# Message stage of two graph layers: weights and the lane row read from PSUM, two sum banks, add ahead of the product

## The chip, the cores and the metric

The kernel runs on one core of one Trainium2 chip. The metric is the device time of one execution in microseconds; lower is better. The core has five engines that run side by side and wait for each other through semaphores: TensorE (PE, its weight loads PEld), VectorE (DVE), ScalarE (ACT), GpSimd (POOL) and SyncE (SP). SBUF and PSUM are its memories of 128 partitions.

## The reference

The model runs four layers over 2500 nodes with 256 features: a graph attention layer (4 heads), a mixture of experts, a graph transformer layer (8 heads) and a second mixture. The two graph layers use 80,000 edges, sorted by destination. What this case touches is the last step of each graph layer: every edge takes its source's row, scales each head's part by the edge's attention weight, and the results are summed per destination.

```python
ex = jnp.exp(scores - m[edge_dst])                 # layer 0, 4 heads of 64
denom = jax.ops.segment_sum(ex, edge_dst, num_segments=N)
alpha = ex / jnp.maximum(denom[edge_dst], 1e-09)
msg = alpha[:, :, None] * h[edge_src]
agg = jax.ops.segment_sum(msg, edge_dst, num_segments=N)
# layer 1, 8 heads of 32, the same with a self loop on each node
msg = Vh[src] * a[:, :, None]
attn = jax.ops.segment_sum(msg, dst, num_segments=N).reshape(N, D_MODEL)
```

## The kernel before, in words

Edges are cut into 157 groups of 512 (four tiles of 128 edges, one edge on a partition), nodes into 20 tiles of 128. Because the edges are sorted, a group touches one node tile or a few; the pairs of group and tile form a staircase of NS = 176 steps, and a table `s.steps` tells each step its ring slot, tile and group. The table row of a node holds 256 values and a one behind each head (D + H = 260 or 264 columns), so that the denominators are summed along; the division comes later.

`pass_messages` is the message stage, once for each graph layer (in layer 0 `most` is None, in layer 1 it holds each node's self loop weight). Its engines:

- GpSimd (`gather_quad`, L731) fetches table rows with indirect DMAs (L756), 128 rows each, eight to a quad (two groups). A ring holds 8 quads (RQ). For quad q it waits at L1034 until the product of the last step on quad q - 8 has been made. Seven quads (layer 0) or eight (layer 1) are gathered before the stage starts. In the ring turns 1 to 5 (layer 0) or 1 to 8 (layer 1) every second quad isn't gathered: it was gathered during the score stage (`gather_ahead`, L795) and stored in HBM, and SyncE loads it with one DMA (L1057). The offsets of a gather lie in SBUF (`g.index`).
- SyncE (`report`) waits for landed rows (L1063) and tells VectorE through `rows_landed`.
- VectorE, for step n: the one-hots `pick` of the four tiles (L1094: destination minus tile base, compared with the row 0..127; 512 columns), a wait for the rows, the product `msg` (L1098: ring rows times weights; 1040 or 1056 columns), and then the add of the sums of step n - LATE (LATE = 2) from PSUM into `acc` in SBUF (L1107: 260 or 272 columns).
- TensorE multiplies one-hots by messages, four fp32 matmuls a step (L1121), into one of DEPTH = 3 PSUM banks `ps_m`.
- ScalarE, in layer 1 only, copies the self loop weights into the tail of `msg` (L1077).

`pick` and `msg` have three buffers each. `staged` unrolls the steps six at a time. In layer 0 the weights lie in spare columns of `xn` (tile name all_xn), in layer 1 in a tensor of their own (e_weight). `lane_row`, `dst_col` and `tile_base` lie in SBUF.

## Time and profile before

| | us |
|---|---|
| median of 3 runs | 3143.92 |
| lowest, highest run | 3139.3, 3148.53 |
| profiled execution | 3144.7 |
| its span, first to last instruction | 3142.8 |
| message stage of layer 0, first one-hot to the next stage's first VectorE instruction | 554.23 to 1202.80 |
| message stage of layer 1, likewise | 2287.20 to 2817.53 |
| busy in the whole span: PE, DVE, ACT, POOL | 1798.8, 1769.9, 368.8, 1701.8 |
| mean granted TensorE clock, as a share of 2.4 GHz | 0.764 |

The profile is one execution. A timeline line gives start and duration in us, the engine, the line of the kernel, the operation and what it writes and reads; in brackets stands the engine's idle time before it and what ended it. A group line gives the count, the busy time in us, the mean of one in ns, and the idle time before its members. "issue" is time in which the engine waited for nothing that the profile shows.

### The profile page before, as it was taken

How to read it: one execution, taken by the hardware profiler on the slowest of the kernel's cores; microseconds unless marked ns; L12 is line 12 of the kernel's file. 1: busy time of each engine (PE TensorE's matmuls, PEld its weight loads, DVE VectorE, ACT ScalarE, POOL GpSimd, SP SyncE). 2: the span in 40 equal slices, each digit the busy share in tenths (PEclk: the TensorE clock that was granted, in tenths of full speed). 3: DMA queues.
4: the chain of work that ended last, by engine and by line, in shares of the span. 5: the costliest groups of instructions: out<-in, count | busy, mean ns of one | idle time of the engine just before them, and what ended most of it. 6: DMA issues, size and time to landing. Idle time of an engine off the chain costs nothing. (4 is left out here: it accounts for less than half of the span.)

```text
span 3142.8 us, 35335 instructions
## 1 busy us (share of the span) xinstructions
PE 1798.8 (57%) x10362; PEld 1444.4 (46%) x10362; DVE 1769.9 (56%) x2713; ACT 368.8 (12%) x715; POOL 1701.8 (54%) x1504
## 2 busy tenths in 40 slices
PE   2301292777755553999741112693177777756668
PEld 2200182555544442799740000693155555535557
DVE  6200098867644447455730000699787777757756
ACT  1100001000000001445200000000300000004244
POOL 3577606887877775000047777205878788761010
PEclk8655596888877776899865555797588888878889
DMA  3355553455433332000135566433145554430000
GB/s 121 119 190 189 173 184 95 126 160 162 136 92 92 92 91 74 1 1 0 63 89 196 196 200 198 148 117 112 54 146 165 162 165 162 134 115 8 4 31 34
DMA packets 140778, 361.01 MB, mean 115 GB/s; under 512 B 39352, under 2 KB 65360, under 8 KB 126890
## 3 DMA queue, kind: packets, MB, share of 16 engines
q0 software_dynamic: 69760, 225.91, 24.0%
q1 hardware_dynamic: 65866, 122.18, 11.2%
q10 hardware_dynamic: 5088, 12.13, 1.1%
q8 instruction: 32, 0.52, 0.1%
q14 instruction: 32, 0.26, 0.0%
HBM read 289.00 MB, written 71.12 MB: 115 GB/s over the span
## 5 line engine op out<-in xcount | busy, mean ns | idle before, releaser
L756 POOL DMA_INDIRECT e_ring<-table,e_index x840 | 1101.4, 1311 | 369.7 <-issue 255.5
L1121 PE MATMUL ms_ps_m<-ms_msg,ms_pick 128*128 128x260 f32 (+1 forms) x2816 | 830.4, 461 | 373.0 <-issue 258.2
L1121 PEld LDWEIGHTS ms_ps_m<-ms_msg,ms_pick 128*128 128x128 f32 x2816 | 634.4, 230 | 568.8 <-issue 432.3
L657 PE MATMUL sc_ps_e<-sc_keys,sc_hot 125*128 125x100 bf16 (+1 forms) x3840 | 353.7, 240 | 569.5 <-issue 561.3
L620 DVE TENSOR_REDUCE all_xn<-sc_ps_e 128x800 f32 (+1 forms) x240 | 234.1, 1019 | 633.7 <-remote 527.8
L657 PEld LDWEIGHTS sc_ps_e<-sc_keys,sc_hot 125*128 125x128 bf16 x3840 | 272.7, 102 | 650.3 <-issue 633.3
L795 POOL DMA_INDIRECT all_acc<-table,e_stage_index x416 | 397.1, 955 | 142.4 <-issue 141.1
L1098 DVE TENSOR_TENSOR ms_msg<-e_ring,all_xn 128x1040 f32 x176 | 218.0, 1239 | 254.1 <-SPq L1063 135.6
L1098 DVE TENSOR_TENSOR ms_msg<-e_ring,e_weight 128x1056 f32 x176 | 220.9, 1255 | 128.1 <-SPq L1063 112.7
L1094 DVE SCALAR_TENSOR_TENSOR ms_pick<-graph_dst_col,graph_tile_base,graph_lane_row 128x512 f32<-128x512 f32 x352 | 263.7, 749 | 12.0 <-issue 9.8
L1107 DVE TENSOR_TENSOR all_acc<-all_acc,ms_ps_m 128x260 f32 (+1 forms) x352 | 150.3, 427 | 8.3 <-PE ms_ps_m L1121 8.0
L131 POOL TENSOR_TENSOR w_qkv_low<-w_qkv,w_qkv_high 128x1536 fp32r<-128x1536 f32 x1 | 3.7, 3657 | 278.4 <-ACT w_qkv_high L126 278.4
L887 ACT ACTIVATE all_acc<-wt_ps_t 128x512 f32<-128x512 f32 x15 | 8.0, 624 | 1001.4 <-PE wt_ps_t L860 1001.3
L131 DVE TENSOR_TENSOR moe_hidden_low<-all_acc,moe_hidden_high 128x512 fp32r<-128x512 f32 x80 | 55.2, 692 | 94.7 <-ACT moe_hidden_high L126 94.7
L728 POOL COPY e_index<-graph_src_col 128x32 int32 (+1 forms) x40 | 14.4, 359 | 158.1 <-SPq L847 158.0
L1077 ACT ACTIVATE ms_msg<-e_dst_line 128x32 f32 x176 | 40.6, 231 | 499.8 <-PE ms_ps_m L1121 433.9
L140 PE MATMUL moe_ps_y<-moe_w_high,moe_hidden_high 128*128 128x256 f32 x320 | 91.4, 286 | 1.9 <-DVE moe_hidden_low L131 1.9
L140 PE MATMUL moe_ps_y<-moe_w_high,moe_hidden_low 128*128 128x256 f32 x320 | 91.6, 286 | 0.0
L140 PE MATMUL moe_ps_y<-moe_w_low,moe_hidden_high 128*128 128x256 f32 x320 | 91.5, 286 | 0.0
L419 ACT ACT_TABLE_LOAD x3 | 3.8, 1283 | 680.8 <-PEq L1142 670.8
L614 DVE TENSOR_SCALAR sc_hot<-sc_rows,all_node_of 125x1024 bf16<-125x1024 bf16 x160 | 80.7, 506 | 4.3 <-DMA sc_rows<-src_low 4.1
L446 PE MATMUL ln_ps_t<-all_ident,all_xn 128*128 128x128 f32 x160 | 31.2, 365 | 85.9 <-DVE all_xn L409 78.0
(415 smaller groups left out, 2682.0 us busy)
## 6 DMA issues: line engine op xcount, KB each, us to landing
ahead<-all_acc POOLq DMA_DIRECT2D x32, 1056.0 KB
e_ring<-ahead SPq DMA_DIRECT2D x32, 1056.0 KB
sc_rows<-src_low SPq DMA_DIRECT2D x160, 200.0 KB
ahead<-all_acc POOLq DMA_DIRECT2D x20, 1040.0 KB
e_ring<-ahead SPq DMA_DIRECT2D x20, 1040.0 KB
e_ring<-table,e_index POOLq DMA_INDIRECT x840
sc_rows<-src_high ACTq DMA_DIRECT2D x160, 50.0 KB
all_acc<-table,e_stage_index POOLq DMA_INDIRECT x416
```

What stands on the lines that cost most here:

```text
L131: return dve.tensor_tensor(low, value, high.bitcast(F32), ALU.subtract)
L140: product = pe.matmul(out, a, b, start=first and i == 0, stop=last and i == len(products) - 1)
L614: dve.tensor_scalar(hot[0:KEYS, q, :], rows[0:KEYS, q, :], s.node_of[0:KEYS, 0:1], None, ALU.is_equal).then_inc(hot_ready, 1)
L620: dve.tensor_reduce(edge[:, bass.ds(it * ITEM + sub * SL, SL), :], found, AX.X, ALU.max).then_inc(picked, 1)
L657: mm = pe.matmul(ps_e[lane][:, t * SLOT:t * SLOT + C], hot[0:KEYS, q, cols], keys[0:KEYS, part, :, :].rearrange("p g h -> p (g h)"), start ...
L756: pool.indirect_dma_start(out=g.ring[:, slot * QUAD + i // GT, i % GT, :], out_offset=None, in_=s.table[:, :], in_offset=bass.IndirectOffs ...
L795: pool.indirect_dma_start(out=stage.rows[:, b, t, :], out_offset=None, in_=s.table[:, :], in_offset=bass.IndirectOffsetOnAxis(ap=stage.ind ...
L1077: act.activation(msg[:, b, :, R:W], most[:, bass.ds(group * GT, GT), :], ACT.Copy).then_inc(tail_ready, 1)
L1094: dve.scalar_tensor_tensor(out=pick[:, b, :, :], in0=s.dst_col[:, bass.ds(group * GT, GT)].unsqueeze(2).broadcast_to([P, GT, P]), scalar=s ...
L1098: dve.tensor_tensor(msg[:, b, :, 0:R].rearrange("p t (h o) -> p t h o", h=H), ring[:, bass.ds(slot, 1), :, :].rearrange("p a t (h o) -> p ...
L1107: dve.tensor_tensor(into, into, ps_m[(b - LATE) % DEPTH][:, 0:W], ALU.add).then_inc(added, 1)
L1121: mm = pe.matmul(ps_m[b][:, 0:W], pick[:, b, t, :], msg[:, b, t, :], start=t == 0, stop=t == GT - 1)
```

## The change

The row 0..127 is copied once into a PSUM bank (`ps_lane`) by ScalarE, and the one-hots read it there. In layer 0 ScalarE copies all weights (2560 columns, five banks) into PSUM once; in layer 1, where they don't fit, it copies those of each step (32 columns) into one of three banks, ahead of its tail copy, and VectorE waits for them (`weight_set`). Products read the weights there. The sums use two banks in place of three. VectorE's step becomes one-hots, add of step n - 2, wait for rows, product. `iteration` now gets the step's position in the unrolled loop (q), from which buffer b = q % DEPTH and bank q % BANKS follow.

```diff
--- before.py
+++ after.py
@@ -978,7 +978,13 @@
         ring, row_in, order = g.ring, g.row_in, g.order
         pick = m.sb("pick", [P, DEPTH, GT, P])
         msg = m.sb("msg", [P, DEPTH, GT, W])
-        ps_m = [m.ps(f"ps_m{i}", [P, 512]) for i in range(DEPTH)]
+        BANKS = 2
+        ps_m = [m.ps(f"ps_m{i}", [P, 512]) for i in range(BANKS)]
+
+        ps_lane = m.ps("ps_lane", [P, 512])
+        lane_row = ps_lane[:, 0:P]
+        ps_w = m.ps("ps_w", [P, ET, H]) if most is None else [m.ps(f"ps_w{i}", [P, 512]) for i in range(DEPTH)]
+        near_set, weight_set = m.sem("near_set"), m.sem("weight_set")
         rows_landed, ahead_in, loaded, most_kept = m.sem("rows_landed"), m.sem("ahead_in"), m.sem("loaded"), m.sem("most_kept")
         acc_zero, tail_ready, pick_ready, msg_ready, summed, added = (
             m.sem(n) for n in ("acc_zero", "tail_ready", "pick_ready", "msg_ready", "summed", "added"))
@@ -1016,12 +1022,12 @@
             unroll = 2 * DEPTH
             first = DEPTH + (NS - DEPTH) % unroll
             for n in range(first):
-                iteration(n, n % DEPTH, n)
+                iteration(n, n, n)
             with eng.Fori(0, (NS - first) // unroll) as turn:
                 for q in range(unroll):
-                    iteration(turn * unroll + (first + q), (first + q) % DEPTH, None)
+                    iteration(turn * unroll + (first + q), first + q, None)
             for n in range(NS, last):
-                iteration(n, n % DEPTH, n)
+                iteration(n, n, n)
 
         def later(fixed, than):
 
@@ -1070,13 +1076,18 @@
 
             @block.scalar
             def _(act):
-                def iteration(n, b, fixed):
+                def iteration(n, q, fixed):
+                    b = q % DEPTH
                     (group,) = step_values(ENG.Activation, n, slice(2, 3), (NG - 1,))
                     if later(fixed, DEPTH):
                         act.wait_ge(summed, n - (DEPTH - 1))
+                    act.activation(ps_w[b][:, 0:GT * H].rearrange("p (t h) -> p t h", h=H), weight[:, bass.ds(group * GT, GT), :], ACT.Copy).then_inc(weight_set, 1)
                     act.activation(msg[:, b, :, R:W], most[:, bass.ds(group * GT, GT), :], ACT.Copy).then_inc(tail_ready, 1)
 
-                if most is not None:
+                act.activation(lane_row, s.lane_row[:, :], ACT.Copy).then_inc(near_set, 1)
+                if most is None:
+                    act.activation(ps_w[:, :, :], weight[:, :, :], ACT.Copy).then_inc(weight_set, 1)
+                else:
                     act.wait_ge(most_kept, 1)
                     staged(act, iteration, NS)
 
@@ -1086,39 +1097,50 @@
                 if most is not None:
                     dve.tensor_tensor(most, most, s.is_last[:, :].unsqueeze(2).broadcast_to([P, ET, H]), ALU.mult).then_inc(most_kept, 1)
                 dve.wait_ge(acc_zero, 2)
-
-                def iteration(n, b, fixed):
+                dve.wait_ge(near_set, 1)
+                if most is None:
+                    dve.wait_ge(weight_set, 1)
+
+                def iteration(n, q, fixed):
+                    b = q % DEPTH
                     slot, tile, group, tile_late = step_values(ENG.DVE, n, slice(0, 4), (RING - 1, NT - 1, NG - 1, NT - 1))
                     if fixed is None or fixed < NS:
 
                         dve.scalar_tensor_tensor(out=pick[:, b, :, :], in0=s.dst_col[:, bass.ds(group * GT, GT)].unsqueeze(2).broadcast_to([P, GT, P]),
-                                                 scalar=s.tile_base[:, bass.ds(tile, 1)], in1=s.lane_row[:, :].unsqueeze(1).broadcast_to([P, GT, P]),
+                                                 scalar=s.tile_base[:, bass.ds(tile, 1)], in1=lane_row.unsqueeze(1).broadcast_to([P, GT, P]),
                                                  op0=ALU.subtract, op1=ALU.is_equal).then_inc(pick_ready, 1)
-                        dve.wait_ge(rows_landed, group + 1)
-                        dve.tensor_tensor(msg[:, b, :, 0:R].rearrange("p t (h o) -> p t h o", h=H),
-                                          ring[:, bass.ds(slot, 1), :, :].rearrange("p a t (h o) -> p (a t) h o", h=H),
-                                          weight[:, bass.ds(group * GT, GT), :].unsqueeze(3).broadcast_to([P, GT, H, O + 1]), ALU.mult).then_inc(msg_ready, 1)
                     if later(fixed, LATE):
 
                         dve.wait_ge(summed, n - (LATE - 1))
                         if later(fixed, LATE + 1):
                             dve.wait_ge(added, n - LATE)
                         into = acc[:, bass.ds(tile_late, 1), 0:W].rearrange("p a w -> p (a w)")
-                        dve.tensor_tensor(into, into, ps_m[(b - LATE) % DEPTH][:, 0:W], ALU.add).then_inc(added, 1)
+                        dve.tensor_tensor(into, into, ps_m[(q - LATE) % BANKS][:, 0:W], ALU.add).then_inc(added, 1)
+                    if fixed is None or fixed < NS:
+                        dve.wait_ge(rows_landed, group + 1)
+                        if most is None:
+                            shares = ps_w[:, bass.ds(group * GT, GT), :]
+                        else:
+                            dve.wait_ge(weight_set, n + 1)
+                            shares = ps_w[b][:, 0:GT * H].rearrange("p (t h) -> p t h", h=H)
+                        dve.tensor_tensor(msg[:, b, :, 0:R].rearrange("p t (h o) -> p t h o", h=H),
+                                          ring[:, bass.ds(slot, 1), :, :].rearrange("p a t (h o) -> p (a t) h o", h=H),
+                                          shares.unsqueeze(3).broadcast_to([P, GT, H, O + 1]), ALU.mult).then_inc(msg_ready, 1)
 
                 staged(dve, iteration, NS + LATE)
 
             @block.tensor
             def _(pe):
-                def iteration(n, b, fixed):
+                def iteration(n, q, fixed):
+                    b = q % DEPTH
                     pe.wait_ge(pick_ready, n + 1)
                     pe.wait_ge(msg_ready, n + 1)
                     if TAILS:
                         pe.wait_ge(tail_ready, n + 1)
-                    if later(fixed, DEPTH):
-                        pe.wait_ge(added, n - (DEPTH - 1))
+                    if later(fixed, BANKS):
+                        pe.wait_ge(added, n - (BANKS - 1))
                     for t in range(GT):
-                        mm = pe.matmul(ps_m[b][:, 0:W], pick[:, b, t, :], msg[:, b, t, :], start=t == 0, stop=t == GT - 1)
+                        mm = pe.matmul(ps_m[q % BANKS][:, 0:W], pick[:, b, t, :], msg[:, b, t, :], start=t == 0, stop=t == GT - 1)
                     mm.then_inc(summed, 1)
 
                 staged(pe, iteration, NS)
```

## Rows read from the trace of the kernel before

**Rows 1.** the page, part 5: out<-in xcount | busy us, mean ns | idle before it

```profile
L795 POOL DMA_INDIRECT all_acc<-table,e_stage_index x416 | 397.1, 955 | 142.4 <-issue 141.1
```

**Rows 2.** groups by line, 550 to 1203 us, message stage of layer 0

```profile
L756 POOL DMA_INDIRECT e_ring<-table,e_index x412 | 512.3, 1244 | 125.1 <-issue 124.4 <-DMA e_ring<-table,e_index 0.6
L1121 PE MATMUL ms_ps_m<-ms_msg,ms_pick 128*128 128x260 f32 x1408 | 427.9, 473 | 225.7 <-issue 135.7 <-DVE ms_msg L1098 56.3 <-DVE all_acc L1107 33.1
...
L1098 DVE TENSOR_TENSOR ms_msg<-e_ring,all_xn 128x1040 f32 x176 | 218.0, 1239 | 254.1 <-SPq L1063 135.6 <-issue 118.5
L1094 DVE SCALAR_TENSOR_TENSOR ms_pick<-graph_dst_col,graph_tile_base,graph_lane_row 128x512 f32<-128x512 f32 x176 | 131.8, 749 | 5.9 <-issue 4.3 <-DVE all_acc L1085 0.8
L1107 DVE TENSOR_TENSOR all_acc<-all_acc,ms_ps_m 128x260 f32 x176 | 74.1, 421 | 3.2 <-PE ms_ps_m L1121 3.1
```

**Rows 3.** the same for 2287 to 2820 us, message stage of layer 1

```profile
L756 POOL DMA_INDIRECT e_ring<-table,e_index x308 | 417.8, 1357 | 105.7 <-issue 94.9 <-DVE ms_msg L1098 10.5 <-DMA e_ring<-table,e_index 0.3
...
L1098 DVE TENSOR_TENSOR ms_msg<-e_ring,e_weight 128x1056 f32 x176 | 220.9, 1255 | 128.1 <-SPq L1063 112.7 <-issue 15.3
...
L1107 DVE TENSOR_TENSOR all_acc<-all_acc,ms_ps_m 128x272 f32 x176 | 76.3, 433 | 5.1 <-PE ms_ps_m L1121 4.9
```

**Rows 4.** timeline (start us, us, engine, line) of one stretch of layer 0

```profile
700.93 0.75 DVE L1094 SCALAR_TENSOR_TENSOR ms_pick<-graph_dst_col,graph_tile_base,graph_lane_row 128x512 f32<-128x512 f32 x1
701.59 1.24 DVE L1098 TENSOR_TENSOR ms_msg<-e_ring,all_xn 128x1040 f32 x1
701.81 1.85 POOL L756 DMA_INDIRECT e_ring<-table,e_index  x1 [0.30 <-issue]
...
703.08 0.75 DVE L1094 SCALAR_TENSOR_TENSOR ms_pick<-graph_dst_col,graph_tile_base,graph_lane_row 128x512 f32<-128x512 f32 x1
703.96 0.94 POOL L756 DMA_INDIRECT e_ring<-table,e_index  x1 [0.30 <-issue]
705.21 0.95 POOL L756 DMA_INDIRECT e_ring<-table,e_index  x1 [0.30 <-issue]
```

**Rows 5.** timeline: a gather that begins inside a one-hot, one inside an add

```profile
764.55 0.75 DVE L1094 SCALAR_TENSOR_TENSOR ms_pick<-graph_dst_col,graph_tile_base,graph_lane_row 128x512 f32<-128x512 f32 x1 [0.46 <-issue]
764.88 1.24 POOL L756 DMA_INDIRECT e_ring<-table,e_index  x1 [0.30 <-issue]
...
766.37 0.42 DVE L1107 TENSOR_TENSOR all_acc<-all_acc,ms_ps_m 128x260 f32 x1
766.43 0.95 POOL L756 DMA_INDIRECT e_ring<-table,e_index  x1 [0.30 <-issue]
```

**Rows 6.** groups of VectorE by shape, whole span

```profile
L957 DVE SCALAR_TENSOR_TENSOR all_xn<-e_dst_line,all_xn 128x2560 f32<-128x2560 f32 x2 | 9.6, 4797 | 0.1
...
L1629 DVE SCALAR_TENSOR_TENSOR all_acc<-dense_ps,w_b,all_acc 128x512 f32<-128x512 f32 x10 | 7.5, 750 | 8.9 <-PE dense_ps L140 8.9
```

**Rows 7.** stretches: us, busy us of each engine (instructions), granted clock, DMA share, GB/s

```profile
570.00:600.00 30.00, 26.76 (x108) 19.14 (x106) 27.70 (x39) 0.00 (x0) 25.87 (x16) 1.00 0.41 134
554.00:850.00 296.00, 222.90 (x816) 176.42 (x817) 224.02 (x308) 0.00 (x0) 242.29 (x184) 0.86 0.48 150
1810.00:1980.00 170.00, 32.28 (x110) 11.72 (x110) 12.05 (x15) 0.00 (x0) 126.63 (x151) 0.50 0.62 199
```

**Rows 8.** one line: duration ns min/median/max, first and last start

```profile
L891 ACT ACTIVATE all_acc<-all_acc x3: 2337/2339/2339, 541.1 to 2257.7; 128x2560 f32<-128x2560 f32 x3
```

**Rows 9.** timeline of ScalarE in layer 1, backlogged TensorE ahead of it

```profile
2297.02 0.23 ACT L1077 ACTIVATE ms_msg<-e_dst_line 128x32 f32 x1 [1.60 <-PE ms_ps_m L1121]
```

**Rows 10.** timeline: the end of the message stage of layer 0

```profile
1192.43 1.85 POOL L756 DMA_INDIRECT e_ring<-table,e_index  x1 [0.31 <-issue]
...
1202.80 0.24 DVE L1146 TENSOR_SCALAR fin_inv<-all_acc 128x80 f32<-128x80 f32 x1 [0.50 <-PEq L1030]
```

**Rows 11.** timeline: the end of the message stage of layer 1

```profile
2807.11 1.87 POOL L756 DMA_INDIRECT e_ring<-table,e_index  x1 [0.30 <-issue]
...
2817.53 0.24 DVE L1544 TENSOR_SCALAR dense_loop<-all_score 128x160 f32<-128x160 f32 x1 [0.33 <-PEq L1030]
```

## The prediction

> **What bounds the kernel now.** Read the groups by line of the two message stages first, then a stretch of the timeline, then the two ends. A stage has 176 steps; VectorE spends 0.75 us of each on one-hots, 1.24 or 1.26 on the product and 0.42 on the add, and sits idle 254 us (layer 0) and 128 us (layer 1) before products, mostly until SyncE reports landed rows (L1063) [rows 2, 3]. So rows come too slowly, and these come from GpSimd's indirect gathers at L756: 412 of them in layer 0, 308 in layer 1, with only 0.30 us between two [rows 2 to 4]. GpSimd is never out of work: its idle time is that issue gap, and once 10.5 us for a ring place [rows 2, 3]. It sets the end of both stages: the last gather ends at 1192.43 + 1.85 = 1194.28, 8.5 us before the next stage's first VectorE instruction, and at 2807.11 + 1.87 = 2808.98, also 8.5 us before it [rows 10, 11].
>
> The gathers themselves are slow here. They take 1.244 us and 1.357 us on average, where the same kind of instruction takes 0.955 us in the score stages [rows 1 to 3]. The timeline says which are slow. The one at 701.81 begins inside a product and ends at 703.66, which is 0.83 us after that product's end (701.59 + 1.24); the two behind it, with VectorE idle, take 0.94 and 0.95 [rows 4]. One that begins inside a one-hot ends at 766.12, 0.82 us after it; one that begins 0.06 us into an add takes 0.95 [rows 5]; of 19 that begin inside an add none is longer than 0.98. So a gather needs something at its start that a product or a one-hot holds to its end and an add does not. Product and one-hot read two tensors from SBUF; the add reads one from SBUF and one from PSUM. While VectorE works without pause, each 2.15 us step (700.93 to 703.08) holds one gather of 1.85 + 0.30 us [rows 4]: both are locked together, though a free gather needs 0.95 + 0.30 = 1.25 us.
>
> **Part 1, the second operand moves to PSUM (one-hot: lane row; product: weights).** If the held thing is what the second SBUF tensor takes, all gathers fall to 0.955 us. Layer 0: 512.3 − 412 × 0.955 = 118.8 us. Layer 1: 417.8 − 308 × 0.955 = 123.7 us. The issue gaps stay. The sum, 242.5 us, comes off the path if GpSimd still sets both ends.
>
> Does it? In layer 0 its last gather would end at 1194.3 − 118.8 = 1075.5, while VectorE needs 176 × 2.15 = 378 us from 554 on, so 143 us are to spare. In layer 1 it would end at 2685.3 and the stage 8.5 us later at 2693.8. VectorE's step there is 2.15 + 0.016 + 0.012 = 2.18 us (longer product and add), so 384 us from 2287.2, with some 6 us of issue gaps as in layer 0 [rows 2, 3], and about 6 us for the last sums: 2683. Only 11 us are left, and the ring ties the two, as a gather waits for the product eight quads back. Every second quad comes from the HBM copy until turn 8, so a quad pair costs GpSimd 8 × 1.26 = 10.1 us and VectorE, at 176/157 steps a group, 4.5 × 2.18 = 9.8. I charge 4 us for stalls of this tie (0 if they never meet, 11 if VectorE sets the end).
>
> Does an operand in PSUM make VectorE slower? For 260 columns the add, with a PSUM operand, takes 421 ns; for 1040 the product, without, takes 1239: 1.05 ns a column, and the same 150 ns fixed [rows 2]. The one-hot has its twin at L1629: 512 columns, a per-partition scalar, one tensor in PSUM, 750 ns against 749 [rows 2, 6]. So nothing. By the Trainium skill (VectorE: DVE Perf Modes, section on the TRN2 errata) an instruction that reads PSUM pays 120 cycles where one from SBUF pays 58, so 65 ns more, twice a step; by that table layer 1's step would be 2.31 us and the stage end at 2706. The trace does not agree: its pairs differ by 1 ns.
>
> What no row shows is a PSUM operand that repeats each value (the weights, 65 or 33 times over). Lower bound: no extra. Upper bound: the strided read at L957, 4797 ns for 2560 columns, 1.81 ns a column after 150 fixed [rows 6]; for the product that is +0.79 us. I take nothing, since the product already repeats the weights from SBUF at 1.05.
>
> **Part 2, ScalarE's copies into PSUM.** Layer 0: one copy of 2560 columns at 2.34 us [rows 8] beside the two engines' memsets, ahead of the first one-hot at 554; hidden. If ScalarE began late, at most 2.3 us once. Layer 1: 176 copies of 16 to 32 columns, near the tail copy's 0.23 us. ScalarE has 1.60 us of idle even while TensorE steps at 0.23 + 1.60 = 1.83 us [rows 9]. The first product waits for one more copy: 0.4 us. Later ones need step n − 3 summed; the product of n comes 5.3 us after that of n − 3 ended, against 1.83 for the sums and 0.5 for both copies. Uncovered, they would put 0.2 us on each step.
>
> **Part 3, the order one-hot, add, product.** No instruction is added on VectorE but one wait. Behind the add's wait for the sums of n − 2 now stand the product and, through it, TensorE, the ring place and GpSimd. From the end of product n − 2 to that add lie one-hot, add and product of n − 1 and the one-hot of n: 2.15 + 0.66 − 0.09 = 2.7 us. The sums take 1.83 plus some 0.2: 0.6 us spare. Before, the product lay between as well, 1.15 us more. In return the add no longer stands behind the wait for rows, and TensorE's 33 us of waiting for adds in layer 0 [rows 2] go; they hide behind the gathers, so nothing.
>
> **Part 4, two banks.** TensorE's step n waits for add n − 2, which VectorE now does before product n, and TensorE waits for that anyway. Nothing. The faster gathers raise the traffic: 184 gathers in 296 us made 150 GB/s at a DMA share of 0.48 [rows 7]; at 1.26 us it becomes some 210 GB/s. The score stage ran 199 GB/s at 0.62 with gathers undisturbed at 0.955 [rows 1, 7]. Nothing.
>
> **Sum.** 118.8 + 123.7 − 4 − 0.4 = 238 us. The profiled run took 3144.7 us (span 3142.8), so 2906.7; the median of the runs is 0.8 below it: 2906 us. Within the case 2890 (no stalls, gathers at 0.945 us, 5 us of spread between runs) to 2920 (the full 11 for the tie, ScalarE's 2.3, the spread).
>
> **Rivals.**
> A. One-hots still hold the gathers, since the per-partition scalar is read from SBUF beside dst_col. Then in unbroken work two steps (4.30 us) hold three gathers, 1.43 us each, +0.18. Alternating turns: 160 + 256 gathers, 75 us; the rest, one one-hot a step with half of them met for 0.3 us, 15 us. GpSimd's slowness then gives VectorE pauses, so about 80: 2986. For: a pointer is an SBUF read. Against: it is 128 single values, in about 60 ns (749 against 512 × 1.04 + 150).
> B. A PSUM read costs VectorE something fixed. Up to 0.06 us a step (11/176) it hides in layer 1; twice that, 0.12 us, puts VectorE's end at 2704, 10 us past GpSimd's where I charged 4: 2912. Against: the pairs above. The skill's table named there is this case.
> C. The sums come late. TensorE's granted clock is 1.00 in unbroken work and 0.86 over the busy part of layer 0 [rows 7], full and half rate (2.4 and 1.2 GHz) mixed, after gaps without rows. At half rate a step is twice 1.83, 1.8 us too many, of which 0.6 are spare. If this hits once in every six steps of layer 1: 29 × 1.2 = 35, less the 11 spare, in place of the 4: 2926. Against: the gaps go as gathers speed up.
> D. The product's repeated PSUM read runs at the strided rate: step 2.15 + 0.79 = 2.94 us, VectorE sets both ends. Layer 0: 176 × 2.94 + 12 = 529 us for now 648.6; layer 1: 535 for 530.3. Together −115: 3029.
> E. Slower than before: both repeated operands run at 1.81 or worse. One-hot +0.39 too, step 3.33 us in layer 0, 3.36 in layer 1: 598 + 603 = 1201 us against 1179, so 3166. It decides from a step of 3.28 us, 1.1 more than now. Against: both repeat from SBUF at full rate.
> F. The change doesn't do what it says: what blocks is the long write or the length of the product, not its second SBUF input. Then 3144. Against: the one-hot, only 0.75 us, holds a gather to its end, and the add holds none.
>
> **Chances.** Forecast 0.72, A 0.10, B 0.03, C 0.04, D 0.04, E 0.04, F 0.03. The range from 2890 takes in A and ends at 2990; D, E and F stay out, 0.11. Less than 0.3% (9 us) is about what a measurement of this kernel can't tell from nothing. Faster: 0.93; same: 0.03 (F); slower: 0.04 (E).
>
> **What would show it.** Gathers at L756 with a mean near 0.955 and hardly any above 1.0; 40 of them in 50 us where now 31 stand; last gathers near 1075 and, counted from the start of layer 1's stage, near 398 us in. Product 1.24 and one-hot 0.75 unchanged (B, D, E if not). Idle before the product in layer 0 small until about 780 us, then 5 us a quad; in layer 1 close to none before the product and little before the add (C if much). Slow gathers that end 0.82 us after a one-hot are A, after a product F. I am wrong outright if gathers are short and the stages still don't shrink: then DMA landing sets the pace.

## The result

The changed kernel took 3301.5 us (median of four, 3290 to 3311), the kernel before 3142.9 us beside it: a ratio of 1.050, interval 1.046 to 1.054. The forecast was 2906 us. One thing must be known for all that follows: one and the same kernel before took some 3140 us in the runs of the result and in those around f1_after, t2_mixed and u1_dose below (*starved* runs from here on), and 2937 us around all other experiments (*free* runs). In free runs the changed kernel takes 2689 us, 8.5% less than the kernel before (2937.1). So the sign of the change hangs on the kind, and the forecast was made from a starved profile.

The page of the changed kernel, part 5 (columns as in [rows 1]; "remote" is a signal whose sender the profile couldn't tell):

```profile
L756 POOL DMA_INDIRECT e_ring<-table,e_index x840 | 854.7, 1018 | 724.9 <-DVE ms_msg L1126 354.4
L1143 PE MATMUL ms_ps_m<-ms_msg,ms_pick 128*128 128x260 f32 (+1 forms) x2816 | 821.8, 446 | 547.5 <-DVE ms_msg L1126 303.5
...
L657 PE MATMUL sc_ps_e<-sc_keys,sc_hot 125*128 125x100 bf16 (+1 forms) x3840 | 351.9, 238 | 575.3 <-issue 564.2
L620 DVE TENSOR_REDUCE all_xn<-sc_ps_e 128x800 f32 (+1 forms) x240 | 230.0, 984 | 635.2 <-remote 417.7
...
L1118 DVE TENSOR_TENSOR all_acc<-all_acc,ms_ps_m 128x260 f32 (+1 forms) x352 | 150.6, 428 | 569.1 <-remote 295.0
L1126 DVE TENSOR_TENSOR ms_msg<-e_ring,ms_ps_w 128x1040 f32 (+1 forms) x352 | 436.2, 1239 | 0.6 <-ACT ms_ps_w L1084 0.4
L1109 DVE SCALAR_TENSOR_TENSOR ms_pick<-graph_dst_col,graph_tile_base,ms_ps_lane 128x512 f32<-128x512 f32 x352 | 261.0, 742 | 0.8 <-DVE all_acc L1096 0.8
```

The same page of the kernel before has for the gathers:

```profile
L756 POOL DMA_INDIRECT e_ring<-table,e_index x840 | 1101.4, 1311 | 369.7 <-issue 255.5 <-SPq L847 101.9 <-DVE ms_msg L1098 10.5
```

The change did to the instructions what it was meant to do. Gathers fell from 1311 to 1018 ns on average, the product still takes 1239, the one-hot 742 (749 in [rows 2]). What is new is 569 us of VectorE idle ahead of the add, and 354 us in which GpSimd waits for products: the ring is full. Groups by line of layer 0's message stage (the same view as [rows 2]):

```profile
L756 POOL DMA_INDIRECT e_ring<-table,e_index x412 | 391.2, 950 | 294.7 <-DVE ms_msg L1126 172.3 <-issue 121.9 <-DMA e_ring<-table,e_index 0.3
...
L1126 DVE TENSOR_TENSOR ms_msg<-e_ring,ms_ps_w 128x1040 f32 x176 | 216.6, 1231 | 0.2 <-issue 0.2
...
L1118 DVE TENSOR_TENSOR all_acc<-all_acc,ms_ps_m 128x260 f32 x176 | 74.3, 422 | 343.9 <-remote 295.0 <-PE ms_ps_m L1143 48.2 <-issue 0.7
```

The wait ahead of the product went from 254.1 us [rows 2] to 0.2, the one ahead of the add from 3.2 to 343.9. The stage grew from 648.1 to 728.8 us (first one-hot to end of last add), layer 1's from 530.0 to 614.6, where the same two waits went from 128.1 to 0.4 and from 5.1 to 225.1 [rows 3]. The two stages make 165 of the 167 us between the spans (3309.8 and 3142.8). A stretch of the timeline shows one such wait (lines left out at the dots):

```profile
996.54 1.91 PE L1143 MATMUL ms_ps_m<-ms_msg,ms_pick 128*128 128x260 f32 x8 [2.36 <-DVE ms_msg L1126]
...
1004.01 1.23 DVE L1126 TENSOR_TENSOR ms_msg<-e_ring,ms_ps_w 128x1040 f32 x1
...
1005.47 3.81 PE L1143 MATMUL ms_ps_m<-ms_msg,ms_pick 128*128 128x260 f32 x8 [7.02 <-DVE ms_msg L1126]
1006.02 0.94 POOL L756 DMA_INDIRECT e_ring<-table,e_index  x1 [1.05 <-DVE ms_msg L1126]
1007.27 0.95 POOL L756 DMA_INDIRECT e_ring<-table,e_index  x1 [0.30 <-issue]
...
1014.79 0.95 POOL L756 DMA_INDIRECT e_ring<-table,e_index  x1 [0.30 <-issue]
1016.99 0.43 DVE L1118 TENSOR_TENSOR all_acc<-all_acc,ms_ps_m 128x260 f32 x1 [11.09 <-remote]
```

The add at 1016.99 takes the sums of the step whose matmuls start at 996.54; as modelled they end at 998.45. VectorE gets their signal 18.4 us later, when GpSimd's series of eight gathers, started 1.25 us apart from 1006.02 on, is over, and stands still for 11.09 us of that; behind the add stand the product, the ring place and GpSimd. The trace has kept the time of 160 of layer 0's 176 signals. Of these, 46 came more than 5 us after the last matmul's modelled end, on average 11.9 and at most 21.6 us: 30 while GpSimd stood still after a series, 16 while gathers still went on. In the kernel before, none of the 323 signals kept in its two message stages came more than 3.5 us late. Since the ends are modelled, the traces don't tell whether the last matmuls or only their signal is late.

### The profile page after: what moved, and what is told of

Its sections match the earlier page's. It is cut to its first block and busy times, and to the rows that moved or that the text cites. A ratio compares the mean times of both kernels' runs of the same rounds, so it can differ in the third digit from the quotient of the medians.

```text
span 3309.8 us, 35845 instructions
## 1 busy us (share of the span) xinstructions
PE 1786.6 (54%) x10362; PEld 1397.2 (42%) x10362; DVE 1768.5 (53%) x2713; ACT 392.2 (12%) x894; POOL 1455.2 (44%) x1504
## 5 line engine op out<-in xcount | busy, mean ns | idle before, releaser
L756 POOL DMA_INDIRECT e_ring<-table,e_index x840 | 854.7, 1018 | 724.9 <-DVE ms_msg L1126 354.4
L1143 PE MATMUL ms_ps_m<-ms_msg,ms_pick 128*128 128x260 f32 (+1 forms) x2816 | 821.8, 446 | 547.5 <-DVE ms_msg L1126 303.5
L1143 PEld LDWEIGHTS ms_ps_m<-ms_msg,ms_pick 128*128 128x128 f32 x2816 | 592.9, 219 | 776.0 <-issue 664.5
L1126 DVE TENSOR_TENSOR ms_msg<-e_ring,ms_ps_w 128x1040 f32 (+1 forms) x352 | 436.2, 1239 | 0.6 <-ACT ms_ps_w L1084 0.4
L1109 DVE SCALAR_TENSOR_TENSOR ms_pick<-graph_dst_col,graph_tile_base,ms_ps_lane 128x512 f32<-128x512 f32 x352 | 261.0, 742 | 0.8 <-DVE all_acc L1096 0.8
L1084 ACT ACTIVATE ms_ps_w<-e_weight 128x32 f32 x176 | 35.4, 201 | 554.5 <-PE ms_ps_m L1143 277.3
L1342 ACT ACTIVATE all_acc<-moe_ps_h,moe_bias 128x512 f32<-128x512 f32 x80 | 55.1, 689 | 119.8 <-PE moe_ps_h L140 119.1
```

What stands on the lines that cost most here:

```text
L756: pool.indirect_dma_start(out=g.ring[:, slot * QUAD + i // GT, i % GT, :], out_offset=None, in_=s.table[:, :], in_offset=bass.IndirectOffs ...
L1109: dve.scalar_tensor_tensor(out=pick[:, b, :, :], in0=s.dst_col[:, bass.ds(group * GT, GT)].unsqueeze(2).broadcast_to([P, GT, P]), scalar=s ...
L1126: dve.tensor_tensor(msg[:, b, :, 0:R].rearrange("p t (h o) -> p t h o", h=H), ring[:, bass.ds(slot, 1), :, :].rearrange("p a t (h o) -> p ...
L1143: mm = pe.matmul(ps_m[q % BANKS][:, 0:W], pick[:, b, t, :], msg[:, b, t, :], start=t == 0, stop=t == GT - 1)
L1342: act.activation(hidden[:, slot, f, :], ps_h[slot * KB + f][:, :], ACT.Gelu, bias=bias[:, j, f:f + 1]).then_inc(hidden_kept, 1)
```

## The experiments

Three theories of the late sums came first. Theory G: gathers that follow each other without a break delay the others' signals, and in the kernel before the products had kept such series short. Theory O: the new order leaves the sums too little room. Theory B: two banks do. The code below is cut to the lines that matter; lines that only rename or set up are left out.

**One part at a time.** e1_order is the kernel before with the add put between one-hot and product (operands in SBUF, three banks). In this cut `product` and `add` stand for their instructions and waits.

```diff
-    product(n); if later(fixed, LATE): add(n - LATE)
+    if later(fixed, LATE): add(n - LATE)
+    product(n)
```

> The kernel before with the new order alone: one-hot, add, product; both operands still in SBUF, three banks. Theory G (free-running gathers delay the sums; products that hold the gathers protected them): the gathers are still held, so the sums come on time and the time stays at 3143 us within 15. Rival O (the order leaves the sums too little room, whatever the gathers do): slower by 60 us or more, VectorE idle ahead of the add.

e2_banks is the kernel before with two banks.

```diff
-        ps_m = [m.ps(f"ps_m{i}", [P, 512]) for i in range(DEPTH)]
+        BANKS = 2
+        ps_m = [m.ps(f"ps_m{i}", [P, 512]) for i in range(BANKS)]
```

> The kernel before with two banks for the sums in place of three, old order, operands in SBUF. Theory G: 3143 us within 15, since TensorE's step waits for an add that comes 0.43 us after the product. Rival B (two banks tie TensorE to VectorE and that makes the sums late): slower by 60 us or more, TensorE idle for the add.

e3_psum is the changed kernel with the product ahead of the add again, the diff above backwards.

> The changed kernel with the old order (one-hot, product, add of two steps before), operands in PSUM, two banks. Theory G: the gathers run free as in the changed kernel (mean about 1.02 us), the sums of the two stages come late in bursts again, and the time stays above 3200 us. Rival O: about 2906 us, what was forecast, since only the order was wrong.

e4_lane is the kernel before with only the row 0..127 in PSUM.

```diff
-                 in1=s.lane_row[:, :].unsqueeze(1).broadcast_to([P, GT, P]),
+                 in1=lane_row.unsqueeze(1).broadcast_to([P, GT, P]),
```

> The kernel before with only the row 0..127 in PSUM: one-hots no longer hold the gathers, products still do; old order, three banks. Theory G: gathers are shorter than 1.25 us and still throttled by one product a step; some gain is left, 3060 to 3143 us, and the sums are late in few places. Rival O and rival B: the same gain, no more late sums than before; should the time rise above 3160, even this much freedom of the gathers costs more than it gives.

Measured, all four beside 2936.5 us for the kernel before, free runs:

| kernel | us | ratio, interval |
|---|---|---|
| e1_order | 2923.7 | 0.9953, 0.9935 to 0.9971 |
| e2_banks | 2930.4 | 0.9982, 0.9971 to 0.9992 |
| e3_psum | 2691.9 | 0.9165, 0.9147 to 0.9182 |
| e4_lane | 2929.4 | 0.9977, 0.9965 to 0.9989 |

O and B fall for free runs: neither order nor banks cost anything, the order gains 13 us. Theory G as I had put it, with late sums and over 3200 us for e3_psum, falls too: its gathers run free and its sums are on time (4.5 and 4.0 us of idle ahead of the adds). The gain needs the weights in PSUM: with the row alone the gathers stay at 1229 and 1371 ns and 7 us are gained, where I had expected up to 83. With VectorE at work each gather of e4_lane still begins inside a product and ends 0.8 us after it: one at 601.87 takes 1.84 us, beside a product at 601.66 of 1.23.

The surprise was the 2936 us, 206 less than the kernel before took beside the result. The score stage says where they went, in groups by line; first the kernel before in the starved run, then e2_banks, whose score stage is the same code, in the free one:

```profile
L795 POOL DMA_INDIRECT all_acc<-table,e_stage_index x159 | 151.8, 954 | 54.5 <-issue 54.0 <-DMA ahead<-all_acc 0.3 <-POOL e_stage_index L781 0.2
L657 PE MATMUL sc_ps_e<-sc_keys,sc_hot 125*128 125x100 bf16 x103 | 24.6, 245 | 196.9 <-issue 196.9
...
L620 DVE TENSOR_REDUCE all_xn<-sc_ps_e 128x800 f32 (+1 forms) x4 | 4.0, 992 | 189.9 <-remote 189.9
```

```profile
L657 PE MATMUL sc_ps_e<-sc_keys,sc_hot 125*128 125x100 bf16 x1416 | 91.7, 241 | 37.0 <-DVE sc_hot L614 36.9
...
L795 POOL DMA_INDIRECT all_acc<-table,e_stage_index x76 | 74.1, 975 | 49.1 <-DMA ahead<-all_acc 29.7 <-issue 18.6 <-DMA all_acc<-table,e_stage_index 0.6
L620 DVE TENSOR_REDUCE all_xn<-sc_ps_e 128x800 f32 (+1 forms) x61 | 59.9, 984 | 3.1 <-PE sc_ps_e L657 3.0
```

In 222 us of the starved run TensorE made 103 matmuls and was idle 196.9 us for "issue", VectorE made 4 reduces; in 130 us of the free run it was 1416 and 61. From its first weight load to its last reduce that stage took 387.7 us against 164.3, layer 1's 547.6 against 194.9. Only part of this shows in the total, since in free runs the end of the score stage doesn't set when the message stage starts: in e1_order GpSimd still makes 66 gathers from 310 to 400 us, with no matmul beside them. Layer 0's message stage starts at 477.9 us in e2_banks where the starved run has 554.2, layer 1's at 2076.0 where it has 2287.2: 76 us in the one layer and 135 more up to the other. The message stages of the kernel before hardly differ between the kinds (648.1 and 530.0 us starved, 647.2 and 531.8 in g2_score below, a free run in which they are the old code). And the starvation goes with GpSimd's gathers: the starved run made 159 of them in those 222 us, and from 400 to 480 us, with none, even it made 1401 matmuls.

**The same kernels in starved runs.** Theory S: what starves the score stage also delays the sums. f1_after is the changed kernel.

> The changed kernel itself, once more. In the four runs before, the kernel before took 2936 us, 207 us less than in the runs shown with the change, and in the score stage TensorE was not left idle for issue. Theory S (sums come late only where something outside the kernel also starves the score stage): where the kernel before takes 2936 us, this one takes about 2695 us, as the version with the old order did (2692); where it takes 3143 us, 3300. Rival O (the new order is the cause, everywhere): about 5% slower than the kernel before in either surrounding, so some 3080 us beside 2936.

f2_three has the old order, both operands in PSUM and three banks in both layers (ScalarE copies the shares step by step in layer 0 too).

```diff
-        BANKS = 2
+        BANKS = 3
-        ps_w = m.ps("ps_w", [P, ET, H]) if most is None else [m.ps(f"ps_w{i}", [P, 512]) for i in range(DEPTH)]
+        ps_w = [m.ps(f"ps_w{i}", [P, 512]) for i in range(DEPTH)]
```

> Operands in PSUM, old order, three banks for the sums in both layers (the shares copied step by step in layer 0 too). Theory S: beside 2936 us, no more than 10 us under the version with two banks (2692), for there VectorE waits 8.6 us for sums in all; beside 3143 us it is the version that suffers least from late sums, since a sum may be one step later: under 3200 us. Rival O: 2692 us or less beside 2936.

These runs were starved (kernel before 3133.9 us, 3070 to 3145). The changed kernel took 3271.7 (4.4% more than the kernel before), f2_three 3315.7. So with the old order and three banks the loss is the same or larger: O and B fall in starved runs as well. f2_three's message stages have 325.3 and 207.2 us of idle ahead of the adds. I had expected less than 3200 and was wrong: a step more of room, 2.15 us, doesn't help against delays of 12 us.

**Rate or bytes.** Theory I: it is GpSimd's issue of gathers, their rate, that starves the others (what is left of G). Theory T: the bytes they bring do. g0_after is the changed kernel again; g1_spaced puts a GpSimd memset behind each gather of the message stages, g2_score does so in the score stages of the kernel before. (Once a quad GpSimd also waits for its memsets.)

```diff
         pool.indirect_dma_start(out=g.ring[...], ...).then_inc(g.row_in[slot % SETS], 16)
+        pool.memset(g.gap[:, i, :], 0.0).then_inc(g.gap_set, 1)
```

g3_narrow gathers 65 (33) numbers a row in the changed kernel. It leaves out the rest of each row, so its output isn't the model's; the same holds for s2_narrow and for layer 0 of t1_mixed and t2_mixed.

```diff
-    pool.indirect_dma_start(out=g.ring[:, ..., :], out_offset=None, in_=s.table[:, :],
+    pool.indirect_dma_start(out=g.ring[:, ..., 0:g.head], out_offset=None,
+        in_=s.table.rearrange("n w -> (n w)")[0:NP * g.head].rearrange("(n w) -> n w", w=g.head),
```

> The changed kernel itself, as the measure for the two that follow and for the surroundings. Theory S (what starves the score stage also delays the sums): beside 3140 us for the kernel before, 3270 us within 40; beside 2936 us, about 2695 us.

> The changed kernel with a GpSimd memset of 256 elements behind each gather of the message stages, so that gathers start about every 1.6 us in place of 1.25. Where the kernel before takes 3140 us: theory G (gathers back to back delay the sums) expects VectorE's 552 us ahead of the adds to fall below 150 and the time to be 3270 us or less, although 840 gathers are 0.35 us further apart; a rival by which the delay has nothing to do with the rate of the gathers expects up to 290 us more than the changed kernel, 3300 to 3560. Where the kernel before takes 2936 us both expect more than the changed kernel, up to 2950 us.

> The kernel before with the same memset behind each gather of the score stages alone (416 of them). Where the kernel before takes 3140 us: theory G expects TensorE and VectorE to be starved less in the score stage and the time to fall, to 3080 us or below; the rival expects no gain, up to 60 us more. Where it takes 2936 us both expect 2936 us or up to 100 us more.

> The changed kernel, in which a gather of the message stages brings 65 of 260 numbers a row in layer 0 (33 of 264 in layer 1), and the product reads these for every head: the same number of gathers at the same places, a quarter to an eighth of their bytes. Where the kernel before takes 3140 us: theory I (it is GpSimd's making and issuing of the gathers that delays the others) expects the changed kernel's time within 40 us; theory T (it is the rows' traffic) expects the sums on time and 2950 us or less. Where it takes 2936 us both expect the changed kernel's time or a little less.

The runs were free: before 2937.1, g0_after 2689.2 (ratio 0.9148, 0.9124 to 0.9172), g1_spaced 2898.1, g2_score 3020.9, g3_narrow 2686.1. The three once more:

> The spaced version once more, for the surroundings in which the kernel before takes 3140 us. Theory G (gathers back to back starve the others there): VectorE's wait ahead of the adds under 150 us, 3270 us or less in all. The rival (their rate has nothing to do with it): 3300 to 3560 us. If the kernel before takes 2936 us again: 2898 us, as before.

> The version whose message gathers bring 65 (33) numbers a row, once more; its output differs for that. Where the kernel before takes 3140 us: theory I (issue of the gathers) expects 3270 us within 40, theory T (their bytes) 2950 us or less. Where it takes 2936 us: 2686 us.

> The kernel before with the memset behind each gather of the score stages, once more. Where the kernel before takes 3140 us: theory G expects 3080 us or less, the rival 3140 to 3200. Where it takes 2936 us: 3021 us.

Free again, with 2899.2, 2688.7 and 3017.0 us beside 2937.9. That tells nothing of the starvation, but the cost of the memsets alone (209 and 84 us), and that three quarters of the gathers' bytes and more are worth no more than 3 us where the sums are on time. Groups of g0_after's two message stages:

```profile
L756 POOL DMA_INDIRECT e_ring<-table,e_index x411 | 390.3, 950 | 125.0 <-issue 123.1 <-DVE ms_msg L1126 1.5 <-DMA e_ring<-table,e_index 0.3
...
L1118 DVE TENSOR_TENSOR all_acc<-all_acc,ms_ps_m 128x260 f32 x176 | 73.6, 418 | 31.0 <-PE ms_ps_m L1143 30.8
```

```profile
L756 POOL DMA_INDIRECT e_ring<-table,e_index x308 | 292.6, 950 | 106.7 <-issue 93.9 <-DVE ms_msg L1126 12.8
...
L1118 DVE TENSOR_TENSOR all_acc<-all_acc,ms_ps_m 128x272 f32 x176 | 75.3, 428 | 7.6 <-PE ms_ps_m L1143 7.6
```

So that one profile of a starved run holds every test, t1_mixed and t2_mixed, which are one kernel, carry one test in each of three stages and leave the fourth as it was.

> The changed kernel with one test in each stage: layer 0's score stage with the memset of 256 elements behind each gather, layer 0's message stage with gathers of 65 numbers a row (its output differs for that), layer 1's score stage as it was, layer 1's message stage with the memset behind each gather. Where the kernel before takes 3140 us: theory I (issue of the gathers back to back starves the others) expects TensorE's idle for issue in layer 0's score stage to fall below half of layer 1's, the sums of layer 0's message stage as late as in the changed kernel (stage of 731 us within 30), and those of layer 1's on time (VectorE under 60 us idle ahead of its adds, stage under 560 us where it was 595). Theory T (the rows' bytes) expects layer 0's message stage at 620 us or less, and no cure by the memsets. Where the kernel before takes 2937 us no stage is starved, and the time is some 2800 us: 2689 and half of what the memsets cost there in the message stages (209) and the score stages (84 less half).

> The same kernel with one test in each stage once more, for a chip on which the kernel before takes 3140 us: theory I expects layer 0's score stage (memsets) to be starved less than half as long as layer 1's, layer 0's message stage (a quarter of the bytes) as long as the changed kernel's (731 us within 30), layer 1's message stage (memsets) under 560 us with under 60 us of VectorE idle ahead of the adds. Theory T expects layer 0's message stage at 620 us or less and no cure by the memsets. Where the kernel before takes 2937 us: 2807 us, as before.

t1_mixed was free (2807.3 us beside 2936.5), t2_mixed starved (3138.0 beside 3154.5, one run of each kernel). Lengths of the stages in us, the same kernel in both, with the changed kernel beside them (score stages from first weight load to last reduce, message stages from first one-hot to end of last add):

| stage | its test | starved | free | changed kernel, starved | changed kernel, free |
|---|---|---|---|---|---|
| score, layer 0 | memsets | 218.0 | 166.6 | 392.1 | 171.1 |
| message, layer 0 | quarter of the bytes | 726.5 | 524.5 | 728.8 | 527.1 |
| score, layer 1 | none | 539.9 | 196.7 | 547.4 | 196.6 |
| message, layer 1 | memsets | 486.3 | 485.1 | 614.6 | 405.8 |

Every line is as theory I has it. A quarter of the bytes changes nothing; the memsets take away most of one score stage's starvation and all of one message stage's, while the score stage without them stays starved in the same execution. The groups of t2_mixed: first its spaced score stage, then the message stages of layer 0 (few bytes) and layer 1 (spaced):

```profile
L657 PE MATMUL sc_ps_e<-sc_keys,sc_hot 125*128 125x100 bf16 x1845 | 122.6, 231 | 65.4 <-issue 44.3 <-DVE sc_hot L614 19.9
```

```profile
L762 POOL DMA_INDIRECT e_ring<-table,e_index x412 | 390.2, 947 | 298.1 <-DVE ms_msg L1142 178.5 <-issue 119.2 <-DMA e_ring<-table,e_index 0.3
...
L1134 DVE TENSOR_TENSOR all_acc<-all_acc,ms_ps_m 128x260 f32 x176 | 74.0, 420 | 342.4 <-remote 295.2 <-PE ms_ps_m L1160 40.5 <-issue 6.2
```

```profile
L762 POOL DMA_INDIRECT e_ring<-table,e_index x308 | 294.8, 957 | 86.8 <-issue 73.5 <-DVE ms_msg L1142 12.2 <-POOL e_gap L766 1.0
...
L766 POOL MEMSET e_gap<- 128x256 bf16 x308 | 101.0, 328 | 0.2
L1134 DVE TENSOR_TENSOR all_acc<-all_acc,ms_ps_m 128x272 f32 x176 | 75.8, 430 | 19.5 <-PE ms_ps_m L1160 18.5 <-issue 0.7
```

The idle ahead of the adds is 342.4 us in the one and 19.5 in the other. Of the signals that the trace kept, 42 of 155 came more than 5 us late in layer 0 and none of 151 in layer 1. Spaced and starved, layer 1's stage is even 44 us shorter than in the kernel before (530.0): with nothing late, the operands in PSUM pay.

**How far apart.** u1_dose, v1_dose and v2_all have the memsets in all four stages, with other sizes (`self.pause` elements in place of 256).

> The changed kernel with a shorter memset behind each gather: 16 elements in layer 0's score stage and layer 1's message stage, 64 elements in layer 1's score stage and layer 0's message stage (256 made one gather start every 1.45 us in place of 1.25 in the message stages, and cured them). Where the kernel before takes 3140 us: if it is the rate (a start every 1.25 us is too often), 16 elements leave the rate almost as it is and cure little: layer 0's score stage stays over 330 us (388 before, 218 with 256), layer 1's message stage over 560 us (615, 486), and 64 elements cure in part. If any other instruction of GpSimd between two gathers is enough, layer 0's score stage takes 250 us or less and layer 1's message stage 420 to 450 us, which would beat the kernel before everywhere. Where the kernel before takes 2937 us it tells the cost alone: 2689 to 2800 us.

Starved: 3197.4 us beside 3143.4, so 1.7% more than the kernel before (interval 0.6 to 2.9, from two runs). In the message stages one gather starts every 1.258 us with 16 elements and every 1.278 with 64 (medians), and the stages shrink little against the changed kernel: layer 1's message stage takes 602.7 us (615), layer 0's 698.0 (729), the score stages 370.4 (392) and 478.4 (547). Groups of layer 1's message stage:

```profile
L1126 DVE TENSOR_TENSOR all_acc<-all_acc,ms_ps_m 128x272 f32 x176 | 76.1, 432 | 213.0 <-DMA sc_rows<-src_low 139.7 <-PE ms_ps_m L1151 63.7 <-issue 9.3
L761 POOL MEMSET e_gap<- 128x16 bf16 x308 | 39.7, 129 | 0.2
```

So what counts is how far apart the gathers are, not that some instruction stands between two of them. In the message stages the cure comes between 1.278 and 1.445 us; in the spaced score stage of t2_mixed, with starts 1.51 us apart, it was not complete (218.0 us, free 166.6). Whether it comes at an edge, v1_dose was to show, and v2_all whether all four stages can be cured at once.

> The changed kernel with memsets of 128 elements in layer 0's score stage and layer 1's message stage, of 192 in layer 1's score stage and layer 0's message stage: in the message stages gathers should start about every 1.33 and 1.39 us (1.278 with 64, 1.445 with 256). Where the kernel before takes 3140 us: if the cure comes with the rate in proportion, layer 1's message stage lies near 555 us (615 without, 486 with 256) and layer 0's near 660 (728 without). If there is an edge between 1.28 and 1.45 us, one of the two is cured (VectorE under 80 us idle ahead of the adds) and the other hardly (over 180 us). Where it takes 2937 us it shows the cost of the memsets alone, 2760 to 2880 us.

> The changed kernel with spaced gathers in all four stages: memsets of 224 elements in the message stages, 256 in the score stages. Where the kernel before takes 3140 us: theory I expects all four stages cured and about 2975 us (3138 of the run with one test in each stage, less 88 for layer 0's message stage at 638 us, less 75 for layer 1's score stage), so 5% under the kernel before and 9% under the changed one. The rival, by which the cures seen were chance or belong to single stages, expects 3100 us or more. Where it takes 2937 us: 2898 and 84 less what 32 elements save, some 2970 us, slower than both kernels there.

Both free: 2904.4 and 2958.5 us beside 2937.1. They give the cost only (one gather each 1.336 and 1.387 us in v1_dose, 1.415 in v2_all's message stages), and both questions stay open. Starved, v2_all would take some 2975 us, an estimate: t2_mixed's 3138 less 89 (layer 0's message stage 726.5, spaced 637.9 in g1_spaced) and less 74 (from the first weight load of layer 1's score stage to its message stage 687 us, in g2_score 613). No version seen here is the fastest on both kinds: the changed kernel is in free runs, and a spaced one should be in starved ones.

## Why the prediction was wrong

**Bound and Part 1: right.** Gathers lose their length to the product's second SBUF operand. The whole change is worth 2937.1 - 2689.2 = 248 us in free runs, where 238 were forecast. In free runs, which have no late sums, the two message stages took 647.2 and 531.8 us in g2_score, where they are the old code, and take 527.1 and 405.8 in g0_after: 120.1 and 126.0 us less, forecast 118.8 and 123.7 less 4.4. The last gather of g0_after's layer 0 ends 518.8 us after the first one-hot, forecast 521. No operand in PSUM costs anything, repeated or not: product and one-hot take 1239 and 742 ns, so B, D and E are out. So are A, with 950 ns a gather in both message stages, and F. That a forecast made from a starved profile fits free runs is no luck: the message stages of the kernel before are as long in both kinds.

**Part 2: right.** ScalarE's copies take 201 ns each and 0.4 us of waiting in all.

**Part 3 and rival C: the step that failed.** I gave the sums 1.83 us plus some 0.2, and 0.6 us to spare. That is how free runs go: 31.0 and 7.6 us of idle ahead of adds in g0_after. In starved ones 46 of 160 are over 5 us late in layer 0, and neither order makes room for that. C named the right place and priced it at 20 us, by TensorE's clock; it cost 728.8 - 527.1 = 201.7 and 614.6 - 405.8 = 208.8 us, by another mechanism. Set against the gain of 120.1 + 126.0 = 246 it gives 164 us of loss; the spans show 167. This is what the forecast lacked: a wait for late sums, put at nothing, that cost 411 us.

**Part 4: the sentence that failed.** "The score stage ran 199 GB/s at 0.62 with gathers undisturbed at 0.955 [rows 1, 7]. Nothing." The gathers were undisturbed there; everything else was not. (The sentence before it is off too: [rows 7] counts all of GpSimd's instructions, and 174 of the 184 are gathers, one in 1.70 us; 150 GB/s at one in 1.26 is 202, not 210. Over the first 291 us of the stage it was 178 GB/s in g0_after and 142 in the result's run.) The last line of [rows 7] had it: 110 matmuls and 15 VectorE instructions in 170 us, beside 151 instructions of GpSimd (120 of them gathers), where 184 (174 gathers) in 296 us of the message stage went with 816 matmuls. I read that line for DMA share alone. Its TensorE column says that in a starved run what goes on beside free-running gathers nearly stands still, and the change was to let the gathers of the message stage run free. The page of the kernel before says the same in tenths of 40 slices (part 2):

```profile
PE   2301292777755553999741112693177777756668
...
POOL 3577606887877775000047777205878788761010
```

In eight slices, the 2nd to 5th and the 22nd to 25th, TensorE has 0 to 3 under POOL's 5 to 7. The change removed a brake on the gathers that had been protecting the sums. That the signals came in time before and late after is measured; that the length of the series is what protected them is inferred from the spacing runs. Counted over the rows of layer 0's gathers: before, no series of starts less than 1.35 us apart is longer than 7; in the changed kernel 98% stand in series of eight or more, the longest of 24.

**What would show it.** Right: gathers and operands by the numbers given. The closing condition, short gathers and no shorter stages, came true in starved runs, but the cause that I gave it, landing rows, isn't the one: the idle ahead of the product, which would show that, is 0.2 us.

**Chances.** 0.04 for slower was far too little for a change whose whole gain lies in making one engine run into a regime that the trace shows another stage suffer from.

## What to carry to other kernels

When a change frees one engine, look for a stretch of the old trace in which it already ran free, and read every other engine's column there, not only the one in question. Where an engine is idle for "issue" or "remote" beside it, price that before the gain. And run before and after side by side more than once, at different times: here the same pair gave -8.5% and +5%.

## What the runs showed of the hardware

The two kinds of runs. The medians of the kernel before lie at 3134 to 3154 us or at 2936.5 to 2937.9, with nothing between (a single execution took 3070). It is not a matter of the chip alone: one and the same gave 2938 us and, nine minutes later, 3143. What sets it isn't known.

In the starved score stage TensorE's matmuls and weight loads take turns while GpSimd gathers, with no wait to account for it: from 160 to 352 us some 60% of them start 1.40 us after the one before, some 30% 0.70. The timeline of the kernel before:

```profile
204.35 0.24 PE L657 MATMUL sc_ps_e<-sc_keys,sc_hot 125*128 125x100 bf16 x1 [4.01 <-issue]
...
205.08 0.10 PEld L657 LDWEIGHTS sc_ps_e<-sc_keys,sc_hot 125*128 125x128 bf16 x1 [2.06 <-issue]
...
206.49 0.24 PE L657 MATMUL sc_ps_e<-sc_keys,sc_hot 125*128 125x100 bf16 x1 [1.90 <-issue]
...
207.88 0.10 PEld L657 LDWEIGHTS sc_ps_e<-sc_keys,sc_hot 125*128 125x128 bf16 x1 [2.69 <-issue]
...
208.58 0.24 PE L657 MATMUL sc_ps_e<-sc_keys,sc_hot 125*128 125x100 bf16 x1 [1.85 <-issue]
...
209.98 0.10 PEld L657 LDWEIGHTS sc_ps_e<-sc_keys,sc_hot 125*128 125x128 bf16 x1 [2.00 <-issue]
```

Weight loads start at 205.08, 207.88 and 209.98, matmuls at 206.49 and 208.58; steps of 1.41, 1.39, 0.70 and 1.40 us, multiples of 0.70. The gathers meanwhile keep their 1.25 us. In g0_after, a free run, gathers in series just as close harm nobody: all 352 signals of the message stages come within 0.02 us of the modelled end. Why one gather in 1.25 us holds the others up in starved runs and one in 1.45 doesn't, was not found. No run here separates GpSimd's issuing from the handling of its requests elsewhere; the runs show only that spacing matters and bytes don't.

The Trainium skill (SBUF — State Buffer, Who interferes with whom) has a VectorE instruction with two SBUF inputs contend with a GpSimd instruction that reads SBUF, and one with at most one, outside the 2-port modes, not. The traces agree: 1244 and 1357 ns a gather beside products with two (1234 and 1352 in e2_banks, a free run), 950 beside products with one. The same section says of TensorE and ScalarE that they never wait on anyone. That may hold for the port, which no run here tests; beyond it the traces don't agree. In starved runs TensorE was idle for issue for 196.9 us beside gathers 1.25 us apart, and for 44.3 beside spaced ones in t2_mixed.
